# A second row buffer, a merged residual and q products ahead of p products in the stage between SAGE and convolution

## What is computed

```python
def _sage_layer(x, src, dst, Wl_i, bl_i, Wr_i):
    msg = x[src]
    agg = segment_sum(msg, dst)
    mean = agg / clip(cnt, 1.0)[:, None]
    return mean @ Wl_i + bl_i + x @ Wr_i        # relu after layers 0 and 1

x1 = _layernorm(x + sage(x))                     # the stage of this change
z = concatenate([x1[dst], x1[src], edge_attr])
msg = sigmoid(z @ Wf.T + bf) * softplus(z @ Ws.T + bs)
agg = segment_sum(msg, dst)
...
```

## Time and profile before

| what | value |
|---|---|
| median of 3 runs | 4452.11 us (4451.31 to 4452.33) |
| profiled execution, its own time | 4451.97 us |
| its span, first to last instruction | 4450.2 us |
| SAGE gathers, third layer | 2124.0 to 3117.2 us of the span |
| the stage between: first L1284 to the last q copy | 3129.78 to 3218.92 us |
| first instruction of the convolution after the q write | 3223.32 us |
| granted TensorE clock, mean of the span | 0.674 |

### The profile page before, as it was taken

The page is one execution under the profiler, slowest core; times in us unless marked ns, Lnnn a source line. Parts: engine busy times, 40 slices in busy tenths (PEclk is TensorE's granted clock), DMA queues, the critical chain, the costliest instruction groups (busy, mean ns, idle before and its releaser), DMA issues.

```text
span 4450.2 us, 57625 instructions
## 1 busy us (share of the span) xinstructions
PE 2487.4 (56%) x11759; PEld 2021.7 (45%) x11760; DVE 1961.4 (44%) x4062; ACT 1138.1 (26%) x2187; POOL 3082.0 (69%) x3220
## 2 busy tenths in 40 slices
PE   4444445555444445556344444455688888888870
PEld 3334444445333344445333444445555555555550
DVE  3222222224122222224333332222678888888877
ACT  1000000001000000001000000000478888888864
POOL 3777777775777777774677777777077777777750
PEclk8555555567555555557555555555899999999995
DMA  6111111112111111111333332111144444444430
GB/s 200 53 53 52 52 52 52 52 53 65 53 53 53 52 52 52 52 52 54 101 103 106 111 110 71 52 52 52 60 131 126 126 127 127 125 127 127 126 84 29
DMA packets 292199, 359.74 MB, mean 81 GB/s; under 512 B 174421, under 2 KB 222958, under 8 KB 291887
## 3 DMA queue, kind: packets, MB, share of 16 engines
q0 software_dynamic: 115728, 264.72, 20.7%
q1 hardware_dynamic: 174096, 90.83, 7.0%
q10 hardware_dynamic: 2352, 3.95, 0.3%
HBM read 314.20 MB, written 52.19 MB: 82 GB/s over the span
## 4 chain that ended last, share of the span: by engine, by line
POOL 56%; issue 32%; DMA 4%; PE 3%; DVE 3%; ACT 1%; POOLq 1%; ACTq 0%; SPq 0%; DVEq 0%
POOL gath L478 41%; POOL gath L497 15%; DMA gath<-y_dram,idx 2%; PE ps L620 1%; DMA y_dram<-work 1%; PE ps L643 1%; ACT work L828 0%; DMA pq<-in_dstT 0%; PE ps L707 0%; PE ps L713 0%; POOLq L475 0%; PE ps L591 0%; DVE mv L1254 0%; DVE st_b L1250 0%; ACT work L804 0%
## 5 line engine op out<-in xcount | busy, mean ns | idle before, releaser
L478 POOL DMA_INDIRECT gath<-y_dram,idx x2352 | 2233.9, 950 | 852.3 <-issue 840.4
L591 PE MATMUL ps<-gath,work 128*128 x5952 | 1420.5, 421 | 1567.5 <-ACTq L778 1433.5
L591 PEld LDWEIGHTS ps<-gath,work 128*128 128x128 f32 x5952 | 1258.1, 316 | 1730.2 <-issue 1730.1
L1156 DVE TENSOR_TENSOR acc<-acc,ps 128x129 f32 x744 | 215.5, 290 | 2180.6 <-PE ps L591 2135.9
L497 POOL DMA_INDIRECT gath<-q_dram,idx x832 | 825.0, 992 | 267.5 <-issue 253.1
L775 ACT COPY idx<-srcT_sb 128x4 int32 (+1 forms) x579 | 112.0, 193 | 2794.5 <-DMA gath<-y_dram,idx 2234.2
L1139 DVE SCALAR_TENSOR_TENSOR work<-ps,w_of,dstT_sb 128x512 f32<-128x512 f32 x753 | 559.9, 744 | 2.0 <-issue 2.0
L671 PE MATMUL ps<-pq,work 128*128 x1664 | 485.5, 394 | 94.9 <-DVE work L1343 64.7
L671 PEld LDWEIGHTS ps<-pq,work 128*128 128x128 f32 x1664 | 251.3, 191 | 208.1 <-issue 134.9
L1343 DVE TENSOR_TENSOR work<-ps,gath 128x1024 f32<-128x1024 f32 x208 | 253.4, 1218 | 77.5 <-issue 65.6
L1334 DVE TENSOR_TENSOR acc<-acc,ps 128x128 f32 x832 | 235.9, 284 | 92.5 <-PE ps L688 64.5
(11 more groups left out here) (194 smaller groups left out, 1221.5 us busy)
## 6 DMA issues: line engine op xcount, KB each, us to landing
gath<-y_dram,idx POOLq DMA_INDIRECT x2352, 2.5
ea_sb<-ea_parts SPq DMA_DIRECT2D x832, 32.0 KB
ea_parts<-pq SPq DMA_DIRECT2D x128, 196.0 KB, 2.6
gath<-q_dram,idx POOLq DMA_INDIRECT x832, 2.8
y_dram<-work SPq DMA_DIRECT2D x21, 448.0 KB, 3.0
eaT_sorted<-in_eaT SPq DMA_DIRECT2D x2, 3136.0 KB, 20.8
pq<-eaT_sorted SPq DMA_DIRECT2D x16, 392.0 KB, 3.3
q_dram<-work SPq DMA_DIRECT2D x7, 896.0 KB, 4.1
```

Of the source, the lines that this page charges most:

```text
L478: pool.indirect_dma_start(msg[:, u, 0:F], None, y_dram, bass.IndirectOffsetOnAxis(ap=idx[:, u:u + 1], axis=0)).then_inc(s_quad[q], 16)
L591: last = te.matmul(ps[:, i % OHS, 0:FA], lhsT=oh4[:, i % OHS, u, :], rhs=gath[:, bass.ds(places[i] + u * FA, FA)], start=u == 0, stop=u == ...
```

## The change

- `hr_of(it)` names one of two row buffers: `work` from 0 or from 6272, where the one-hots of the SAGE sums were. DVE writes the rows of chunk `it` as soon as chunk `it - 2` is normalised.
- The residual is added once to the whole of `res` ahead of the third layer's sums (one instruction, 128 x 6272, behind L1229); L1288 is gone.
- In `new_x1` DVE does rows, statistics, `add_b1(it - 2)`, the clearing of `acc`, and only then waits for the norm of chunk `it - 1` and makes the coefficients.
- PE does all q matmuls of a chunk (semaphore `x1_q`) and then all p matmuls (`x1_p`).
- ACT does the copies of the transposed rows, Ln and Exp of the next chunk, the four q copies, and then the norm of the next chunk.

```diff
+        def hr_of(it):
+            return work[:, bass.ds(it % 2 * 6272, CW * F)].rearrange("p (u f) -> p u f", f=F)
...
                 for b, wins in enumerate(PAIRS):
                     pe.wait_ge(s["x1_copied"], it * 2 + b // 2 + 1 + 1)
+                    pe.wait_ge(s["q_staged"], it * 4 + b + 1)
+                    for u in wins:
+                        last = te.matmul(ps[:, 2 + b % 2, u % 2 * 2 * F:(u % 2 + 1) * 2 * F], lhsT=hT[:, u, :],
+                                         rhs=w1_sb[:, 2 * F:4 * F], start=True, stop=True)
+                    last.then_inc(s["x1_q"], 1)
+                for b, wins in enumerate(PAIRS):
                     pe.wait_ge(s["p_done"], it * 4 + b + 1)
-                    pe.wait_ge(s["q_staged"], it * 4 + b + 1)
-                    for h in range(2):
-                        for u in wins:
-                            last = te.matmul(ps[:, 2 + b % 2 if h else P_BANKS[b], u % 2 * 2 * F:(u % 2 + 1) * 2 * F],
...
-                    last.then_inc(s["x1_prod"], 1)
+                    for u in wins:
+                        last = te.matmul(ps[:, P_BANKS[b], u % 2 * 2 * F:(u % 2 + 1) * 2 * F], lhsT=hT[:, u, :],
+                                         rhs=w1_sb[:, 0:2 * F], start=True, stop=True)
+                    last.then_inc(s["x1_p"], 1)
...
+            deviation_x1(0)
             norm_x1(0)
             with act.Fori(0, NCH - 1) as it:
-                copy_q(it, False)
-            copy_q(NCH - 1, True)
+                copy_x1(it)
+                deviation_x1(it + 1)
+                copy_q(it)
+                norm_x1(it + 1)
...
+            dve.wait_ge(s["prod_act"], 3 * NCH * 2 + 1)
+            dve.wait_ge(s["prod_dve"], 3 * NCH * 2 + 1)
+            link(v.tensor_tensor(res, res, x_sb[:, :], ALU.add))
...
                 if not isinstance(it, int) or it > 1:
-                    add_b1(it - 2)
-                if not isinstance(it, int) or it > 0:
-                    dve.wait_ge(s["x1_ready"], it)
+                    dve.wait_ge(s["x1_ready"], it - 1)
...
-                link(v.tensor_tensor(hr, hr, chunk(x_sb, it, F), ALU.add))
-                statistics("z", hr, st6, mv, ve)
-                coefficients("z", it, mv, ve, rs, nm)
+                alone(dve)
+                statistics("z", hr_of(it), st6, mv, ve)
+                if not isinstance(it, int) or it > 1:
+                    add_b1(it - 2)
                 v.tensor_copy(acc[:, bass.ds(it * (CW * FA), CW * FA)], zero[:, :].to_broadcast([P, CW * FA]))\
                     .then_inc(s["acc_clear"], 1)
+                if not isinstance(it, int) or it > 0:
+                    dve.wait_ge(s["x1_ready"], it)
+                coefficients("z", it, mv, ve, rs, nm)
```

More of the change, by code:

```diff
@@ L237, in build_gnn @@
             idx_ready landed onehots added_items summed iota_put h_ready h_transposed h_copied
-            prod_act prod_dve var_z rs_z coef_z x1_ready x1_tr x1_copied x1_prod p_done q_staged q_written x_kept acc_clear
+            prod_act prod_dve var_z rs_z coef_z x1_ready x1_tr x1_copied x1_q x1_p p_done q_staged q_written x_kept acc_clear
             ea_in ea_1 ea_r1 ea_2 ea_r2 ea_3 ea_written ea_free we_split we_in
@@ L638, in _ @@
                     pe.wait_ge(s["x1_copied"], it * 2 + b // 2 + 1 + 1)
-                    pe.wait_ge(s["p_done"], it * 4 + b + 1)
-                    pe.wait_ge(s["q_staged"], it * 4 + b + 1)
-                    for h in range(2):
-                        for u in wins:
-                            last = te.matmul(ps[:, 2 + b % 2 if h else P_BANKS[b], u % 2 * 2 * F:(u % 2 + 1) * 2 * F],
-                                             lhsT=hT[:, u, :],
-                                             rhs=w1_sb[:, h * 2 * F:(h + 1) * 2 * F], start=True, stop=True)
-                    last.then_inc(s["x1_prod"], 1)
+                    pe.wait_ge(s["q_staged"], it * 4 + b + 1)
[4 more added lines that the diff above has]
+                for b, wins in enumerate(PAIRS):
+                    pe.wait_ge(s["p_done"], it * 4 + b + 1)
+                    for u in wins:
+                        last = te.matmul(ps[:, P_BANKS[b], u % 2 * 2 * F:(u % 2 + 1) * 2 * F], lhsT=hT[:, u, :],
+                                         rhs=w1_sb[:, 0:2 * F], start=True, stop=True)
+                    last.then_inc(s["x1_p"], 1)
             pe.wait_ge(s["we_in"], 16 * len(EA_GROUPS))
@@ L830, in apply_norm, with deviation_x1 @@
                 return last
+            def deviation_x1(it):
+                inverse_deviation("z", it, ve, rs, ("x1_ready", 0))
             def norm_x1(it):
-                inverse_deviation("z", it, ve, rs, ("x1_ready", 0))
                 act.wait_ge(s["coef_z"], it + 1)
@@ L837, in norm_x1, with copy_x1 @@
                 act.wait_ge(s["x1_tr"], it * 2 + 1)
-                apply_norm(x1c, hr, rs, nm).then_inc(s["x1_ready"], 1)
-            def copy_q(it, last):
-                act.wait_ge(s["x1_prod"], it * 4 + 1)
+                apply_norm(x1c, hr_of(it), rs, nm).then_inc(s["x1_ready"], 1)
+            def copy_x1(it):
+                act.wait_ge(s["x1_p"], it * 4 + 1)
                 for k, wins in enumerate(QUADS):
@@ L845, in copy_q @@
                     sc.copy(hT[:, wins[0]:wins[-1] + 1, :], ps_tr[:, wins[0]:wins[-1] + 1, :]).then_inc(s["x1_copied"], 1)
+            def copy_q(it):
                 act.wait_ge(s["q_free"], it + 1)
@@ L848, in copy_q @@
                     n = len(wins)
-                    if b == 2 and not last:
-                        norm_x1(it + 1)
-                    act.wait_ge(s["x1_prod"], it * 4 + b + 1 + 1)
+                    act.wait_ge(s["x1_q"], it * 4 + b + 1 + 1)
                     sc.copy(q_staged(it % 2, wins[0], n),
                             ps[:, 2 + b % 2, 0:n * 2 * F].rearrange("p (u f) -> p u f", f=2 * F)).then_inc(s["q_staged"], 1)
+            deviation_x1(0)
             norm_x1(0)
             with act.Fori(0, NCH - 1) as it:
-                copy_q(it, False)
-            copy_q(NCH - 1, True)
+                copy_x1(it)
+                deviation_x1(it + 1)
+                copy_q(it)
+                norm_x1(it + 1)
+            copy_x1(NCH - 1)
+            copy_q(NCH - 1)
             def ok(g):
@@ L1243, in _ @@
             inverse_counts(2)
-            dve.wait_ge(s["prod_act"], 3 * NCH * 2 + 1)
-            dve.wait_ge(s["prod_dve"], 3 * NCH * 2 + 1)
-            n_links += 8
+            n_links += 9
             def statistics(k, src_, st, mv_, ve_):
@@ L1270, in newton @@
                 link(v.tensor_tensor(y, y, t, ALU.mult))
-            per = 8
+            per = 7
             def new_x1(it):
@@ L1298, in add_b1 @@
                     n = len(wins)
-                    dve.wait_ge(s["x1_prod"], it * 4 + b + 1 + 1)
+                    dve.wait_ge(s["x1_p"], it * 4 + b + 1 + 1)
                     v.tensor_tensor(
```

4 lines of the change are left out of this document (2 added, 2 removed).

## The result

The changed kernel takes **4441.48 us** (median of 20 executions, 4439.68 to 4444.80) against 4451.53 for the kernel before (20 executions, on the same chip). The ratio is 0.9977, 95% interval 0.9971 to 0.9984: 10 us faster, 0.23%. Its profiled execution took 4441.96 us, its span 4440.2. The prediction was 4437, so it is met to 4.5 us and the sign is right. The median lies 0.5 us above the forecast's own range of 4433 to 4441 and inside the wider one of 4430 to 4444. Not all of its terms were right, and in the stage between the misses cancel.

The account below looks back on a forecast made before the run. POOL bounds the kernel overall, a chain of waits the stage between third layer and convolution. Stage 67.7 against 89.1 us (-21.4), +1.0 for a dip, +5.5 for the gather: -14.9, so 4437 us; range 4433 to 4441, wider 4430 to 4444.

Parts of the forecast that it names:

- The chain of 8.5 us between norms: Stage between third layer and convolution: norm, transposes, copies, q matmuls, q copies, next norm take 8.5 us per chunk.
- First chunk 10.8: Stage's first chunk: 4.91 us to first matmul, q half at low clock 5.2, copy 0.7, in all 10.8.
- Head 5.9: Stage's start: first rows to first norm, 7.06 us less the residual's 1.1, so 5.9.
- Last chunk 8.5: Stage's end: the last chunk, from its norm to its last q copy, takes 8.5 us.
- DVE "should just not decide": DVE's turn in the stage, 8.5 to 9.0 us, about 2 us early, would not set the time within seven chunks.
- the first rival: DVE becomes the stage's bound: rows 2.5 us or more, turn 9.4 to 9.6, total 4442 us; chance 0.12.
- the 1.0 us for a dip: Stage: allowance of 1.0 us for part of one drop of TensorE's clock, added to the total.
- The clock: TensorE in the stage: idle about 0.7 us before transposes instead of 2.44, so the whole clock was expected.
- Last p matmuls and `add_b1` under the q write: Stage's end: they finish about 3 us after the last q copy, covered by the 4.4 us q write.
- The gather under the new instruction, 5.5 us: Third layer's start: the second gather stands until the merged residual instruction on DVE ends, costing 5.5 us.
- does not slip between the two: Third layer's start: if the first gather does not slip between the two long DVE instructions, the loss is 6.7 us.
- Everything else is left as it is: Rest of the kernel, the convolution included: unchanged, no term in the sum.

Follow-up runs that it names:

- the best version here: Changed kernel with the bias addition moved to the kernel's start and DVE's loop over chunks written out: 4422.28 us, against 4452.06 for the kernel before (ratio 0.9935).

## Why the prediction was right, and where it was not

- *The chain of 8.5 us between norms*: right, 8.30 measured. Norm to first q matmul 4.35 (4.45 predicted), q half 3.52 (3.34), from there to the norm 0.43 (0.7).
- *First chunk 10.8*: 9.66. The q half took 4.42, not 5.2: I had put the whole 2.07 us of the low clock into it, and the clock (0.79 on average in it) rose sooner. Head 5.9: 6.04. Last chunk 8.5: 8.27.
- *DVE "should just not decide"*: **wrong**, and the first rival came true in part. Its turn was put at 8.5 to 9.0 and is 9.47: rows 2.52 instead of 2.0, loop start 0.72 instead of 0.3. It loses 1.2 us per chunk to the chain instead of 0.5, so the head start of about 2 us is gone after two chunks, and the last three distances are 8.91, 9.48, 9.49. That costs 3.0 us, as writing the loop out shows. The rival had the turn right, 9.4 to 9.6, and its 4442 is the time that was measured, but that is luck: it had 5 us for DVE, without the head start, and nothing for the convolution. The rows' 2.0 came from the earlier trace rows, with one register instruction fewer each, and I took it although no row had the price of one more; the end of the bound that I did not take, 2.5, was the true one. The error is hidden in the sum: the chain was shorter than put, the first chunk too, and no part of the 1.0 us for a dip was needed, so the stage came out at 68.4 against 67.7 plus 1.0.
- *The clock*: right, whole from the second chunk. The run with p ahead of q bears it out: there the idle time ahead of the transposes is 3.32 us and the clock falls to 0.50; here it is 0.35 to 1.00, and my text had put it at about 0.7.
- *Last p matmuls and `add_b1` under the q write*: right. They end at 3209.46, 3.2 us after the last q copy; the index copy that waits for the write comes at 3210.67.
- *The gather under the new instruction, 5.5 us*: right to the hundredth (6.42 us), and for the stated reason: with one input in PSUM it is gone. By the Trainium skill, page "SBUF — State Buffer", section "Who interferes with whom", a `tensor_tensor` does not hold up descriptor generation, for it takes only the shared read interface and the generation needs the write interface (a reason that is marked there as inferred). The trace disagrees, with 6.42 us against 0.94. The text's 6.7 for the case that the first gather "does not slip between the two" was the wrong alternative for the 7.1 that the layer lost: the first gather ended as it should, and the 1.6 us over the 5.5 lie in the gathers behind.
- *"Everything else is left as it is"*: **wrong**, and the step that failed for the total. The instructions of the convolution are the same, but its gathers meet DVE's differently: +5.2 us up to the last gather, of which the total shows 2.6.

From 4437.1 to 4441.96 it is +1.0 before the layer, +1.6 in the layer, -0.3 in the stage and +2.6 in the convolution. The first two lie within what profiles of the same code differ by.

## What to carry to other kernels

Where POOL's gathers set the time, count the DVE instructions with two SBUF inputs that run beside them, and place the long ones where no gather is due: 6.68 us of DVE cost 5.5 us of POOL, and moving one such instruction to the kernel's start gave it back. Do not read the cost off a gather's own length, though: the first one took 1.25 us longer and delayed nothing. When you add a buffer, work out at once which engine's turn comes next, with the in-loop durations and the loop's own start, and ask what the other engine does under the wait that is left. And cut every result into stretches, the untouched ones too: of the 30 us between the kernel before and the best version here, 8 lay in the convolution, which no line of the change touches.

## What the runs showed of the hardware beyond that

- A gather that begins under a DVE instruction with two SBUF inputs ends 0.81 to 0.82 us after it, whether that is a `tensor_tensor` of 6.69 us or a `scalar_tensor_tensor` of 1.22. The first gather of the third layer began 4.26 to 5.79 us into the long instruction in the profiles here, and the second started 7.80 to 7.82 us after that instruction's start in every one.
- Seven rows instructions (128 x 128) take, with POOL idle, 1.92 us with fixed addresses, 1.98 with the three inputs' addresses from registers and 2.52 with the output's too. Beside POOL's copy they take 2.60 with fixed addresses and 2.51 with the three (where the copy runs from 3164.07 on), so the copy's price does not come on top of the registers'; the fourth register beside the copy was not run.
- From the last DVE instruction of a loop's turn to the first of the next, 0.72 us pass in the stage, 1.25 in the convolution, and 1.11 there in the kernels whose loop over chunks is written out.
